# A third buffer for the radial weights and for the hops' one-hots, and one landing wait per sixteen gathers, in a four-layer graph network

## The chip, the cores and the metric

The kernel runs on one core of one Trainium2 chip. The time is the device time of that core in microseconds, from the start of the program to its end. Lower is better. The times come from repeated executions of one compiled program. The profile comes from one further execution.

## The reference

A graph has 6,250 nodes with 64 features and 200,000 edges (source, target, 32 and 4 edge features, two edge types). Four layers run one after the other, each with a residual and a layer norm:

```python
x = _layernorm(x + _L0_gnn_ref(...))   # radial = silu(edge_attr @ w1 + b1) @ w2 + b2: 1024 weights per edge;
                                       # message = tensor product of x[src], the edge harmonics and these weights;
                                       # segment_sum over dst, divided by the source degree
x = _layernorm(x + _L1_gnn_ref(...))   # relational layer: 8 bases, coefficients by edge type, segment_sum over dst
x = _layernorm(x + _L2_gnn_ref(...))   # h = x @ weight; out = segment_sum(h[row] * norm, col) + bias
x = _layernorm(x + _L3_gnn_ref(...))   # two hops; each gathers head, tail and relation rows, works out
                                       # hyperbolic maps per edge, and sums relu(res) over head
```

What matters here is that every layer gathers a row per edge, works on it, and sums it into the rows of nodes.

## The kernel before

**Edges in order.** A first stage ranks the edges by target and by source and writes them into slots, padded so that a group of 256 slots belongs to one chunk of 128 nodes. There are 1,664 tiles of 128 edges. BT = 16 tiles make a block, so there are 104 blocks. A sum over nodes is a matmul: a one-hot matrix of the edges' lanes (128 edges by 128 nodes, made by VectorE with an is_equal against a row of numbers) is the stationary operand, the messages are the moving one, and VectorE adds the 128 x 64 result to the accumulator of nodes in SBUF.

**Layer one** (product_phase). Four engines work on a block at once:

- SyncE loads the block's edge records (l_rec) when VectorE has given the buffer back (rec_used). In the first 50 blocks it also waits there for the scatters that GpSimd issues (rcb_sent) before it reloads their source, and the load of the next block's records is queued behind that.
- GpSimd copies the indices (line 666), issues 16 indirect DMAs that gather the source rows (line 671), waits for all 16, makes the features feat in eight operations (lines 680 to 687), and in the first 50 blocks issues 16 scatters of other records (line 693).
- TensorE turns four tiles of hidden features at a time (lines 727 and 729; ScalarE copies them out, line 713) and makes the 1,024 radial weights of a tile with four matmuls of 512 columns (line 737, function tile). They go to p_rad, which has two buffers of two PSUM banks; tile j may start when VectorE has read tile j-2 (semaphore tile_done). At the end of a block it makes the first two tiles of the next block, then waits for the block's messages (msg_done) and sums them with 16 products (line 761), which the trace shows as 32 matmuls.
- VectorE multiplies each tile's weights by the features (lines 800 and 802), reduces (line 809), and after 16 tiles makes the messages (lines 841 to 845) and the next block's one-hots (line 793). The sums of the last block are added (line 854) between the tiles 2 to 9 of the next one.

**Layer three** (spread_phase). Per block GpSimd issues 16 gathers (line 1101) and waits after each eight until they have all landed. TensorE sums them (line 1115), VectorE makes one-hots (line 1131) and adds (line 592). There are four buffers of gathered rows and of indices; VectorE copies the indices of block b + 4 when the sums of block b are made (line 1141).

**The hops** (hop_phase, twice). A pass handles 64 tiles in four units of 16, and there are 26 passes in a hop. GpSimd gathers the tail rows (line 1458, a wait after each eight). TensorE picks head and relation rows by matmul (lines 1476 and 1480, function pick), ScalarE copies them out (lines 1516 and 1517), and VectorE works through the hyperbolic formulas. Then, unit by unit, VectorE finishes the messages (lines 1779 to 1787), ScalarE applies the relu (line 1539), VectorE makes two halves of edge one-hots (function hots, line 1587, halves m = 0 to 7) in two buffers, TensorE sums a half as soon as its one-hots stand (line 1494), and VectorE adds unit u - 2 (add_unit, line 592). Half m may be written when the sums of half m - 2 are made (sum_done). After the last unit VectorE prepares the next pass with products of the tails and of the heads (lines 1596 and 1611), for which it waits until ScalarE has copied the picked rows.

The order on each engine is the order in which the code is written; semaphores tie the engines together.

## Time and profile before

| | us |
|---|---|
| median of 3 runs | 23192.35 |
| lowest and highest run | 23182.50, 23208.56 |
| the profiled execution | 23174.65 |
| its span, first to last instruction | 23172.8 |
| VectorE busy | 15518.0 (67%) |
| GpSimd busy | 12776.2 (55%) |
| TensorE busy | 10208.4 (44%) |
| ScalarE busy | 2702.6 (12%) |

No engine is busy all the time, so each stage has to be read for itself. Layer one lies between about 3560 and 10440 us, layer two between 10440 and 13250, layer three between 13640 and 16230, and the two hops between 16470 and 23172. The share of busy time in a window tells which engine is nearest to being the bound of a stage, the list of waits tells what an engine waited for, and the timeline shows in which order it happened.

### The profile page before, as it was taken

How to read it: one execution, taken by the hardware profiler on the slowest of the kernel's cores; microseconds unless marked ns; L12 is line 12 of the kernel's file. 1: busy time of each engine (PE TensorE's matmuls, PEld its weight loads, DVE VectorE, ACT ScalarE, POOL GpSimd, SP SyncE). 2: the span in 40 equal slices, each digit the busy share in tenths (PEclk: the TensorE clock that was granted, in tenths of full speed). 3: DMA queues.
4: the chain of work that ended last, by engine and by line, in shares of the span. 5: the costliest groups of instructions: out<-in, count | busy, mean ns of one | idle time of the engine just before them, and what ended most of it. 6: DMA issues, size and time to landing. Idle time of an engine off the chain costs nothing. (4 is left out here: it accounts for less than half of the span.)

```text
span 23172.8 us, 208220 instructions
## 1 busy us (share of the span) xinstructions
PE 10208.4 (44%) x47565; PEld 6761.2 (29%) x47566; DVE 15518.0 (67%) x25810; ACT 2702.6 (12%) x6634; POOL 12776.2 (55%) x12678
## 2 busy tenths in 40 slices
PE   0033335655555555555666632222234434344333
PEld 0033332222222222222222332222233333233333
DVE  8744447998888888887666521111477777677777
ACT  0011110000000000000000000000122332223322
POOL 0188886666565656644666426665355554455553
PEclk9999996555555555557888755555555555555555
DMA  4033331111111111111111101111422222222222
GB/s 176 21 69 69 70 69 28 24 24 24 23 22 23 22 24 21 24 22 22 24 24 24 17 13 21 21 21 20 59 61 61 56 58 51 58 63 60 57 59 47
DMA packets 1151509, 957.47 MB, mean 41 GB/s; under 512 B 803963, under 2 KB 920315, under 8 KB 1150739
## 3 DMA queue, kind: packets, MB, share of 16 engines
q0 software_dynamic: 419904, 437.84, 11.0%
q1 hardware_dynamic: 730960, 512.22, 8.6%
q8 instruction: 260, 4.26, 0.1%
q14 instruction: 385, 3.15, 0.0%
HBM read 734.68 MB, written 210.63 MB: 41 GB/s over the span
## 5 line engine op out<-in xcount | busy, mean ns | idle before, releaser
L1458 POOL DMA_INDIRECT tail<-ball,h_idx x3328 | 3445.4, 1035 | 3295.5 <-issue 1379.1
L737 PE MATMUL p_rad<-w_stack,hid_t 99*128 99x512 bf16 (+1 forms) x6656 | 3073.8, 619 | 2355.2 <-DVEq L827 1082.5
L1494 PE MATMUL h_sum<-head,h_hot 128*128 128x64 f32 x6656 | 1446.7, 417 | 3475.0 <-ACT head L1539 2117.5
L809 DVE TENSOR_REDUCE red<-prod 128x96 f32<-128x1536 f32 x1664 | 2900.2, 1743 | 3.5
L1494 PEld LDWEIGHTS h_sum<-head,h_hot 128*128 128x128 f32 x6656 | 1414.0, 327 | 3500.3 <-issue 3500.3
L1101 POOL DMA_INDIRECT l_xg<-h_tab,l_idx x1664 | 1573.9, 946 | 1462.7 <-issue 957.6
L338 POOL DMA_INDIRECT rec_a<-rec,slot x1600 | 1988.9, 1243 | 517.0 <-issue 501.4
L693 POOL DMA_INDIRECT rec_b<-l_rcb x1600 | 1929.8, 1206 | 570.9 <-issue 514.6
L932 POOL DMA_INDIRECT l_xg<-x_tab,l_idx x1664 | 1574.2, 946 | 1154.2 <-issue 834.1
L948 PE MATMUL l_sum<-outer,l_hot 128*128 128x512 f32 x3328 | 1684.6, 670 | 971.1 <-DVEq L993 899.5
L737 PEld LDWEIGHTS p_rad<-w_stack,hid_t 99*128 99x128 bf16 (+1 forms) x6656 | 773.3, 132 | 4300.7 <-issue 4298.8
L800 DVE TENSOR_TENSOR prod<-p_rad,feat 128x768 f32<-128x768 f32 x1664 | 1581.4, 950 | 545.4 <-remote 279.1
L671 POOL DMA_INDIRECT l_xg<-in_x,l_idx x1664 | 1581.9, 951 | 524.7 <-issue 475.6
L802 DVE TENSOR_TENSOR prod<-p_rad,feat 128x768 f32<-128x768 f32 x1664 | 1576.1, 947 | 0.0
L1115 PE MATMUL l_sum<-l_xg,l_hot 128*128 128x64 f32 x3328 | 734.1, 422 | 1880.5 <-DMA l_xg<-h_tab,l_idx 1880.5
L358 PE MATMUL p_all<-w_all,kinds 97*125 97x40 f32 x3200 | 691.1, 409 | 1637.7 <-DVEq L413 1637.7
L983 DVE TENSOR_TENSOR outer<-l_pcoef,l_xg 128x1024 f32<-128x1024 f32 x832 | 1015.3, 1220 | 527.4 <-DMA l_xg<-x_tab,l_idx 461.5
L1141 DVE COPY l_idx<-src_a 128x16 uint32 x100 | 18.5, 185 | 1914.0 <-PE l_sum L1115 1355.3
L948 PEld LDWEIGHTS l_sum<-outer,l_hot 128*128 128x128 f32 x3328 | 711.8, 218 | 1943.3 <-issue 1943.3
L1115 PEld LDWEIGHTS l_sum<-l_xg,l_hot 128*128 128x128 f32 x3328 | 717.6, 332 | 1897.1 <-issue 1897.1
L1476 PE MATMUL h_head<-ball_parts,hot_t 128*128 x9984 | 1032.3, 271 | 406.7 <-issue 300.2
L713 ACT ACTIVATE hid_t<-l_turn 96x1024 bf16<-96x1024 bf16 x416 | 424.4, 1020 | 6572.0 <-PE l_turn L729 3956.0
(368 smaller groups left out, 18411.8 us busy)
## 6 DMA issues: line engine op xcount, KB each, us to landing
hot_t<-rows_l SPq DMA_DIRECT2D x208, 512.0 KB
rec_a<-fill SPq DMA_DIRECT2D x128, 728.0 KB, 19.6
l_rec<-rec_a SPq DMA_DIRECT2D x104, 896.0 KB, 4.8
rhot_t<-rows_r SPq DMA_DIRECT2D x208, 384.0 KB
tail<-ball,h_idx POOLq DMA_INDIRECT x3328
t<-in_type SPq DMA_DIRECT2D x100, 500.0 KB
l_xg<-in_x,l_idx POOLq DMA_INDIRECT x1664
l_xg<-x_tab,l_idx POOLq DMA_INDIRECT x1664
```

Source lines behind the costliest of these rows:

```text
L338: pool.indirect_dma_start(rec_a[:, :], bass.IndirectOffsetOnAxis(ap=slot[q][:, j:j + 1], axis=0), rec[q][:, j, :], None).then_inc(sent[q], 16)
L671: pool.indirect_dma_start(xg[q][:, j, :], None, x[:, :], bass.IndirectOffsetOnAxis(ap=idx[q][:, j:j + 1], axis=0)).then_inc(gathered[q], 16)
L693: pool.indirect_dma_start(rec_b[:, :], bass.IndirectOffsetOnAxis(ap=rcb[q][:, j, 3:4].bitcast(U32), axis=0), rcb[q][:, j, :], None).then_i ...
L737: ins = pe.matmul(p_rad[j % 2][:, h * 512:(h + 1) * 512], hid_t[j // 4 % 2][0:K3 + 3 * (1 - i), j % 4, i, :], w_stack[i][0:K3 + 3 * (1 - i ...
L800: ch.step(dve.tensor_tensor(o[:, 0:48, :].rearrange("p (a w) u -> p a w u", a=3), w[:, 0:3], bc(f[:, j, 0:3, :].unsqueeze(2), [P, 3, MUL, ...
L802: ch.step(dve.tensor_tensor(o[:, 48:96, :].rearrange("p (w i) u -> p w i u", i=3), bc(w[:, 3].unsqueeze(2), [P, MUL, 3, MUL]), bc(f[:, j, ...
L809: ch.step(dve.tensor_reduce(red[:, j, :], prod[j % 3][:, :, :], AX, ALU.add))
L932: pool.indirect_dma_start(xg[u][:, j, :], None, table[:, :], bass.IndirectOffsetOnAxis(ap=idx[u][:, j:j + 1], axis=0)).then_inc(gathered[u ...
L948: ins = pe.matmul(p_sum[k % 4][:, :], hot[q][:, 2 * k + j, :], outer[k % 3][:, j, :, :].rearrange("p b d -> p (b d)"), start=(j == 0), sto ...
L1101: pool.indirect_dma_start(xg[u][:, j, :], None, table[:, :], bass.IndirectOffsetOnAxis(ap=idx[u][:, j:j + 1], axis=0)).then_inc(gathered[u ...
L1458: pool.indirect_dma_start(tg[q][:, j, :], None, table[:, :], bass.IndirectOffsetOnAxis(ap=idx[q][:, j:j + 1], axis=0)).then_inc(gathered[q ...
L1494: ins = pe.matmul(p_sum[u % 2][:, j % BT // 2, :], hot[j // HP8 % 2][:, j % HP8, :], hg[:, j, 0:D], start=(j % 2 == 0), stop=(j % 2 == 1))
```

## The change

Three edits that don't touch each other. In layer one p_rad gets a third buffer (all eight PSUM banks are then in use), tile j waits for VectorE's reading of tile j - 3, or for the last tile of the block before in the case of tile 0, and TensorE makes three tiles instead of two of the next block before it turns to the sums. In layer three GpSimd waits once per 16 gathers, and the copies of the indices move from VectorE to ScalarE, which has nothing else to do there. In the hops the one-hots of the edges get a third buffer, so half m waits for the sums of half m - 3.

```diff
-        p_rad = [ps(f"p_rad{q}", [P, COLS]) for q in range(2)]
+        p_rad = [ps(f"p_rad{q}", [P, COLS]) for q in range(3)]
...
-                hold(pe, turn, tile_done, b * BT + (j + 1))
+                hold(pe, turn, tile_done, b * BT + (3 if j == 0 else j if j < 3 else j + 1))
...
-                        ins = pe.matmul(p_rad[j % 2][:, h * 512:(h + 1) * 512], hid_t[j // 4 % 2][0:K3 + 3 * (1 - i), j % 4, i, :],
+                        ins = pe.matmul(p_rad[j % 3][:, h * 512:(h + 1) * 512], hid_t[j // 4 % 2][0:K3 + 3 * (1 - i), j % 4, i, :],
...
                 tile(b, 1)
+                tile(b, 2)
...
-                for j in range(2, BT):
+                for j in range(3, BT):
...
-            dve.sem_inc(tile_done, SEED)
+            dve.sem_inc(tile_done, 3)
...
-                w = p_rad[j % 2][:, :].rearrange("p (a w u) -> p a w u", a=4, u=MUL)
+                w = p_rad[j % 3][:, :].rearrange("p (a w u) -> p a w u", a=4, u=MUL)
...
             act.activation(p_row[:, 0:P], g["row"][:, :], ACT.Copy).then_inc(row_ready, 1)
+            for u in range(4):
+                act.activation(idx[u][:, :], g["src_a"][:, u * BT:(u + 1) * BT], ACT.Copy).then_inc(idx_ready, 1)
+            with act.Fori(0, NB // 4 - 1) as it:
+                for u in range(4):
+                    b = it * 4 + u
+                    hold(act, turn, sum_done, b + 1)
+                    act.activation(idx[u][:, :], g["src_a"][:, bass.ds((b + 4) * BT, BT)], ACT.Copy).then_inc(idx_ready, 1)
...
-                        if j % 8 == 7:
-                            hold(pool, turn, gathered[u], it * (16 * BT) + 16 * (j + 1))
+                    hold(pool, turn, gathered[u], it * (16 * BT) + 16 * BT)
...
-            for u in range(4):
-                dve.tensor_copy(idx[u][:, :], g["src_a"][:, u * BT:(u + 1) * BT]).then_inc(idx_ready, 1)
...
-                if left == 2:
-                    dve.tensor_copy(idx[u][:, :], g["src_a"][:, bass.ds((b + 4) * BT, BT)]).then_inc(idx_ready, 1)
...
-        hot = [sb(f"h_hot{k}" + tag, [P, HP8, P]) for k in range(2)]
+        hot = [sb(f"h_hot{k}" + tag, [P, HP8, P]) for k in range(3)]
...
-                        ins = pe.matmul(p_sum[u % 2][:, j % BT // 2, :], hot[j // HP8 % 2][:, j % HP8, :], hg[:, j, 0:D],
+                        ins = pe.matmul(p_sum[u % 2][:, j % BT // 2, :], hot[j // HP8 % 3][:, j % HP8, :], hg[:, j, 0:D],
...
-                if m >= 2:
-                    dve.wait_ge(sum_done, b * (2 * HU) + (m - 1))
-                ch.do(tt(hot[m % 2][:, :, :], lane3, bc(ends[q][:, 0, z].unsqueeze(2), [P, HP8, P]), ALU.is_equal))
+                if m >= 3:
+                    dve.wait_ge(sum_done, b * (2 * HU) + (m - 2))
+                ch.do(tt(hot[m % 3][:, :, :], lane3, bc(ends[q][:, 0, z].unsqueeze(2), [P, HP8, P]), ALU.is_equal))
```

On TensorE, at the end of a block of layer one (the names carry their buffer numbers: l0_hot0 and l0_sum belong to the block that ends, l0_rec1 and p_rad to the next one), before:

```order
L737 MATMUL p_rad0<-w_stack1,hid_t0 128x512 x2
L727 MATMUL l0_turn<-l0_ident_b,l0_rec1 96x128 [waits l0_kept]
L729 MATMUL l0_turn<-l0_ident_b,l0_rec1 96x128
...
L74 REGISTER_ALU
L737 MATMUL p_rad1<-w_stack0,hid_t0 128x512 [waits l0_tile_done]
L737 MATMUL p_rad1<-w_stack0,hid_t0 128x512
L737 MATMUL p_rad1<-w_stack1,hid_t0 128x512 x2
L761 MATMUL l0_sum<-msg,l0_hot0 128x64 [waits l0_msg_done,l0_added]
L761 MATMUL l0_sum<-msg,l0_hot0 128x64 x15
L74 REGISTER_ALU
L737 MATMUL p_rad0<-w_stack0,hid_t0 128x512 [waits l0_tile_done]
```

The same place now:

```order
L74 REGISTER_ALU
L737 MATMUL p_rad1<-w_stack0,hid_t0 128x512 [waits l0_tile_done]
L737 MATMUL p_rad1<-w_stack0,hid_t0 128x512
L737 MATMUL p_rad1<-w_stack1,hid_t0 128x512 x2
L74 REGISTER_ALU
L737 MATMUL p_rad2<-w_stack0,hid_t0 128x512 [waits l0_tile_done]
L737 MATMUL p_rad2<-w_stack0,hid_t0 128x512
L737 MATMUL p_rad2<-w_stack1,hid_t0 128x512 x2
L762 MATMUL l0_sum<-msg,l0_hot0 128x64 [waits l0_msg_done,l0_added]
L762 MATMUL l0_sum<-msg,l0_hot0 128x64 x15
L74 REGISTER_ALU
```

Tile 2 of the next block, with its wait for tile_done, has moved from behind the sums to ahead of them.

On GpSimd, in layer three (l_xg are the gathered rows, l_idx their indices), two blocks before:

```order
L1101 DMA l_xg<-h_tab,l_idx 128x64 [waits h_idx_ready]
L1101 DMA l_xg<-h_tab,l_idx 128x64 x7
L1101 DMA l_xg<-h_tab,l_idx 128x64 [waits l2_gathered1]
L1101 DMA l_xg<-h_tab,l_idx 128x64 x7
L74 REGISTER_ALU [waits l2_gathered1]
L1101 DMA l_xg<-h_tab,l_idx 128x64 [waits h_idx_ready]
L1101 DMA l_xg<-h_tab,l_idx 128x64 x7
```

and now:

```order
L1109 DMA l_xg<-h_tab,l_idx 128x64 [waits h_idx_ready]
L1109 DMA l_xg<-h_tab,l_idx 128x64 x15
L74 REGISTER_ALU [waits l2_gathered1]
L1109 DMA l_xg<-h_tab,l_idx 128x64 [waits h_idx_ready]
L1109 DMA l_xg<-h_tab,l_idx 128x64 x15
```

The wait in the middle of a block is gone, the one at its end has stayed.

## Rows read from the trace of the kernel before

**Rows 1.** Windows by stage (layer one, layer three); columns stand in the first line.

```profile
core 0: us, PE busy (x) PEld busy (x) DVE busy (x) ACT busy (x) POOL busy (x), PEclk, DMA share, GB/s
3560.00:10440.00 6880.00, 4046.84 (x13112) 1848.47 (x13112) 6167.48 (x6137) 419.25 (x411) 4183.57 (x4400) 0.52 0.13 23
...
13640.00:16230.00 2590.00, 731.34 (x3316) 715.00 (x3317) 431.89 (x1028) 0.00 (x0) 1570.33 (x1661) 0.50 0.14 21
```

**Rows 2.** Groups by line, GpSimd's gathers of layer three and scatters of layer one.

```profile
L1101 POOL DMA_INDIRECT l_xg<-h_tab,l_idx x1664 | 1573.9, 946 | 1462.7 <-issue 957.6 <-DVE l_idx L1123 452.9 <-DMA l_xg<-h_tab,l_idx 52.2
...
L693 POOL DMA_INDIRECT rec_b<-l_rcb x1600 | 1929.8, 1206 | 570.9 <-issue 514.6 <-POOL feat L687 56.3
```

**Rows 3.** Timeline of GpSimd in layer three: start, us, idle before and its releaser.

```profile
15011.35 0.95 POOL L1101 DMA_INDIRECT l_xg<-h_tab,l_idx  x1 [0.30 <-issue]
15014.99 0.94 POOL L1101 DMA_INDIRECT l_xg<-h_tab,l_idx  x1 [2.69 <-issue]
...
15027.42 0.95 POOL L1101 DMA_INDIRECT l_xg<-h_tab,l_idx  x1 [2.74 <-issue]
```

**Rows 4.** Timeline of TensorE in layer one, from a block's end into the next.

```profile
6019.41 1.91 PE L737 MATMUL p_rad<-w_stack,hid_t 99*128 99x512 bf16 x4
6026.33 7.06 PE L761 MATMUL l_sum<-msg,l_hot 128*128 128x64 f32 x32 [5.01 <-DVEq L846]
6033.18 3.58 PE L737 MATMUL p_rad<-w_stack,hid_t 99*128 99x512 bf16 x8
...
6044.20 1.87 PE L737 MATMUL p_rad<-w_stack,hid_t 99*128 99x512 bf16 x4 [1.65 <-DVEq L827]
```

**Rows 5.** Timeline of VectorE in the same block: L800 starts a tile.

```profile
6035.13 0.96 DVE L800 TENSOR_TENSOR prod<-p_rad,feat 128x768 f32<-128x768 f32 x1 [1.51 <-issue]
...
6038.66 0.95 DVE L800 TENSOR_TENSOR prod<-p_rad,feat 128x768 f32<-128x768 f32 x1
...
6042.18 0.95 DVE L800 TENSOR_TENSOR prod<-p_rad,feat 128x768 f32<-128x768 f32 x1
...
6053.64 0.96 DVE L800 TENSOR_TENSOR prod<-p_rad,feat 128x768 f32<-128x768 f32 x1 [4.14 <-remote]
```

**Rows 6.** Timeline of GpSimd in the same block: last gather, then the features.

```profile
6049.86 0.95 POOL L671 DMA_INDIRECT l_xg<-in_x,l_idx  x1 [0.30 <-issue]
6052.39 1.50 POOL L680 TENSOR_TENSOR vec<-l_xg,l_rec 128x768 f32<-128x768 f32 x1 [1.58 <-DMA l_xg<-in_x,l_idx]
```

**Rows 7.** VectorE's waits in layer one, from 3600 to 4880 us: total, times, longest.

```profile
DVE prod L800 <- remote: 3.8, 1, 3.8
```

**Rows 8.** The same from 4950 to 10440 us.

```profile
DVE prod L800 <- remote: 275.2, 73, 4.6
DVE prod L800 <- issue: 109.0, 72, 3.2
```

**Rows 9.** GpSimd in layer one's first blocks: start of a block's index copy.

```profile
3638.29 0.20 POOL L666 CAST l_idx<-l_rec 128x16 uint32<-128x16 f32 x1 [7.05 <-DMA l_rec<-rec_a]
...
3892.56 0.21 POOL L666 CAST l_idx<-l_rec 128x16 uint32<-128x16 f32 x1 [7.10 <-DMA l_rec<-rec_a]
```

**Rows 10.** Timeline of VectorE in a pass of the first hop.

```profile
18126.94 1.23 DVE L1587 TENSOR_TENSOR h_hot<-h_row,h_ends 128x1024 f32<-128x1024 f32 x1 [1.86 <-PE h_sum L1494]
...
18139.64 2.60 DVE L1587 TENSOR_TENSOR h_hot<-h_row,h_ends 128x1024 f32<-128x1024 f32 x2 [6.16 <-PE h_sum L1494]
...
18166.88 2.76 DVE L592 TENSOR_TENSOR acc_nodes<-acc_nodes,h_sum 128x64 f32 x8 [2.98 <-PE h_sum L1494]
...
18193.47 0.69 DVE L1596 TENSOR_TENSOR h_hot<-head,h_rhot 128x512 f32<-128x512 f32 x1 [3.89 <-ACT head L1517]
```

**Rows 11.** TensorE in the same pass, the sums of the second unit.

```profile
18131.29 7.06 PE L1494 MATMUL h_sum<-head,h_hot 128*128 128x64 f32 x32 [2.23 <-issue]
```

**Rows 12.** GpSimd in the same pass, the last gather of an eight.

```profile
18137.09 0.95 POOL L1458 DMA_INDIRECT tail<-ball,h_idx  x1 [0.30 <-issue]
```

**Rows 13.** What VectorE's one-hots of both hops waited for: us, times.

```profile
  PE h_sum L1494: 262.6, 132
```

## Prediction made before the run

> **What bounds the kernel now.** I read the windows by stage first, since the busy shares of the whole span are an average over stages with different limits, and then, for each stage that the change touches, the groups by line, the waits and the timelines of the engines that wait.
>
> Layer three is GpSimd's stage: of 2590 us in the window TensorE is busy 731, VectorE 432 and GpSimd 1570 [rows 1]. The 1664 gathers have 1462.7 us of idle time before them [rows 2]. 452.9 of that is one wait at the start of the stage. The rest, 1009.8, is the 0.30 us that stands before each gather anyway, and the wait for landing after each eight, 2.69 and 2.74 us in the block that I looked at [rows 3].
>
> In layer one VectorE is busy for 6167 of 6880 us [rows 1]. It takes a tile each 3.52 us (6038.66 to 6042.18) and stalls twice in most blocks [rows 5]. The first stall is before tile 2 of a block, 1.51 us: TensorE makes tiles 0 and 1, waits 5.01 us for the messages, makes the sums (6026.33 to 6033.39) and only then tile 2 [rows 4]. The second is before tile 6, 4.14 us, released by something that the profile only calls remote. TensorE's matmuls of that tile end at 6046.07 [rows 4], while VectorE starts at 6053.64 [rows 5]. That moment is 3.78 us after the start of the last of the block's 16 gathers, at 6049.86 [rows 6]. In the later blocks such a wait stands 73 times with 275.2 us, and the late wait for tile 2 72 times with 109.0 us [rows 8]; in the first twenty blocks a remote wait stands once [rows 7]. I read it so: TensorE's signal for a tile whose matmuls end while the gathers are being issued is held until they are through. It fits the times; it isn't shown.
>
> In the first 50 blocks GpSimd issues scatters too. Four blocks take 254.27 us there, 63.6 each, paced by its own round (records in, gathers, features, scatters) [rows 9]. By the blocks that I counted, blocks 21 to 49 take about 67.7 us each: there the gathers have come into step with VectorE's stall. That number is from the whole timeline of the stage, and its own stalls (1.5 and 3.8 us over the 63.6) make nearly the same.
>
> In the hops VectorE has gaps at the one-hots (1.86 us before half 3, 6.16 us before half 4), at the sums of the last unit (2.98) and at the head products (3.89) [rows 10]. Over both hops the one-hots wait 262.6 us for TensorE, 132 times [rows 13]. The matmuls that free half 4's buffer are the first half of the 7.06 us from 18131.29 on [rows 11], so they end near 18134.8; VectorE goes on at 18139.64, 2.55 us after the start of an eight's last gather at 18137.09 [rows 12]. This is the same kind of late signal.
>
> **Layer three's waits.** 1664 gathers in 104 blocks have 104 waits in mid-block and 103 at block ends that count. 1009.8 less 1457 x 0.305 = 444 leaves 565 for 207 waits, 2.73 us each, as the two rows show [rows 3]. A gather without the wait stands 0.30 behind the one before it. So the edit takes 104 x (2.73 - 0.305) = **252 us**. The index copies that move to ScalarE cost nothing: it does nothing in this window [rows 1], and each of its four buffers is refilled three blocks ahead of its use. What is late next? TensorE's sums need 731/104 = 7.0 us of a block, VectorE 4.2, and a block would last 22.2 us, so GpSimd stays the bound. The price on the other side is that 16 gathers in flight might be issued or land more slowly than eight. In layer one 16 gathers run back to back with 0.30 us between them, and the last has landed 2.53 us after its start (6049.86 to 6052.39) [rows 6], against 3.64 from start to next gather after eight in layer three (15011.35 to 15014.99) [rows 3]. So I take the full 252. Its bounds are 104 x 2.2 = 229, if the longer run of gathers makes the one remaining wait 0.23 us longer, and 265, if the mid-block waits are a little longer than those at the ends.
>
> Here the Trainium skill bears on the trace. Its page "DMA: Bandwidth & Descriptors", in the section "Anatomy of one DMA — SWDGE (gpsimd) path", puts a fixed 2.0 us on each DMA that GpSimd issues, most of it the time until the write is confirmed and the semaphore may rise. By that page 104 waits would be worth an estimated 208 us. The rows measure what stands in the way of GpSimd, 2.73 us, and the sum goes by them.
>
> **Layer one's third buffer.** No instruction is added but one wait per block that changes its count; tile 2 of the next block moves ahead of the sums. Does it fit there? With three buffers tile 0 waits for the last product of the block, which is where tile 1 waits today (6019.41). Three tiles of 1.91 us are 5.7 us, and the messages come at 6026.33, 6.9 us later [rows 4]; 1.2 us are left for the turns, which are short. So the sums aren't delayed, and the 1.51 us before tile 2 goes. If the cover were short by 1 us, the sums would start so much later, but VectorE needs them only between its tiles 2 and 9, so nothing waits.
>
> What does the second stall do? VectorE comes to tile 6 some 1.5 us earlier, and with three buffers TensorE makes tile 6 one tile (3.52 us) earlier still, so that its matmuls end near 6041 instead of 6046. I take it that this is early enough to be signalled before the hold. Then tile 7 is the one caught: VectorE wants it one tile later than tile 6 and gets it when the hold ends, at the same distance from the gathers as now. So per stalled block the gain isn't the whole 1.5 + 4.1 but **one tile, 3.52 us**. By stretches:
> - blocks 0 to 20: GpSimd's round of 63.6 us sets the pace, nothing is gained;
> - blocks 21 to 49: from 67.7 down to at best GpSimd's 63.6, 29 x 4.1 = 119 us (3.52 by the rule above and a part of it that the gathers' new place gives back);
> - blocks 50 to 103: no scatters, 54 x 3.52 = 190 us.
>
> Sum **309 us**. The bounds are wide, since the held signal is inferred. If only the wait before tile 2 goes, 103 x 1.5 = 155. If the signal's end alone sets the pace of a block, VectorE arriving earlier only waits longer, and about 20 is left. If the stall is gone altogether, the second half gains 54 x (1.5 + 4.1) = 302 and the middle 119 to 160, up to 460.
>
> **The hops' third buffer.** Half m waits for the sums of half m - 3. The gaps of 1.86 (half 3) and 6.16 us (half 4) go, but half 5 then waits for what half 4 waits for today, the signal at 18139.6. Half 4's one-hots are one of the two in the 2.60 us row [rows 10], so 1.3 us per pass are made beside the wait. By this 52 x 1.37 = 71 us, and with the gap of half 3 fully counted 52 x 3.3 = 172. Against it: later in the pass VectorE waits 2.98 us for TensorE and 3.89 for ScalarE's copy of the head rows [rows 10]. Those are set by TensorE's order and by the gathers, not by VectorE, and swallow what came before them in about half of the passes. The next picks by TensorE aren't earlier when VectorE is. I take **50 us**, with 0 and 172 as bounds.
>
> **The sum.** 252 + 309 + 50 = 611 us. 23174.65 - 611 = 22563.65 for the profiled execution, which lies 17.7 us under the median of the runs and 1.85 over its span. For the median I add the 17.7 back, 22581, and say 22580.
>
> **Rivals.**
> - *Only the wait before tile 2 goes in layer one.* The stall at tile 6 then stays as long as it is, because the hold is tied to VectorE's own place in the block: the gathers start when VectorE gives the records back, and move with it. Gain 155 + 252 + 20 = 427, so 22765. The steady 3.78 us between gather and release speaks for it, the earlier end of tile 6's matmuls against.
> - *The stall of layer one vanishes.* If the hold catches only what ends in the last part of the gathers, and tile 7 slips past as well, then 460 + 252 + 100 = 812, so 22380. For it speaks that tiles 3, 4 and 5 come without a wait while gathers are issued too [rows 5].
> - *The edit in layer one does not do what it says.* The held signal sets the block's period and VectorE only waits longer: 20 + 252 + 20 = 292, so 22900. For it: GpSimd's gathers begin when VectorE has given the buffer back, and the release comes a fixed time behind them. Against it: the 1.51 us stall stands ahead of that point in the block.
> - *Slower.* Sixteen gathers in flight without a wait may be issued at the pace of the scatters of layer one, which also come sixteen in a row, 1206 ns and 0.30 apart [rows 2], against 0.95 and 0.30 [rows 3]. Then 1664 x 0.25 = 416 us are added in layer three and 252 saved, 164 slower. With layer one and the hops swallowed to nothing the time is 23192 + 164 = 23356. From 0.15 us more per gather (252/1664) the edit has lost its gain. Against it: layer one's gathers, sixteen in a row too, take 0.95 [rows 6].
>
> **How the numbers follow.** The case of the sum has 0.50, the rival with only tile 2's wait 0.20, the vanished stall 0.15, the swallowed edit 0.10, the slower one 0.02, and 0.03 is left for mixtures near no change. The predicted time is the first case's. The range runs from 22370, which takes in the vanished stall, to 22830, which takes in the case with only tile 2's wait at its upper bound of the hops' zero (22785) and some of the way to the swallowed edit; what is left out is most of that case, the slower one and tails, under 2 in 10. About 0.2%, 46 us, is what a measurement of this kernel can tell from no change: faster by more than that has 0.96, within it 0.02, slower 0.02.
>
> **What would show it.** In layer three the idle time before the gathers falls from 1463 to about 1210 us, no gap stands in mid-block, the gathers stay at 0.95, and a block lasts 22.2 us. In layer one VectorE has no wait before tile 2 of a block, the stall at tile 6 is gone and one of about 2.6 us stands before tile 7, and the stage is 309 us shorter. If the second stall keeps its 4 us at tile 6, the step on the earlier signal was wrong; if the stage gains nearly nothing, the step that VectorE sets the gathers was. In the hops the one-hots' wait for TensorE falls from 262.6 us by half or more, and the waits at the sums (2.98) and at the head products (3.89) grow. The prediction is wrong as a whole if the gathers' mean duration rises in layer three, or if the wait at a block's end grows by the 2.4 us that the middle one gave.

## The result

The changed kernel took 22420.81 us (median of 4 runs, 22394.77 to 22503.10), the kernel before 23200.46 in the runs beside it (23182.50 to 23209.55). The ratio is **0.967, with a 95% interval from 0.9645 to 0.9697**. The profiled execution went from a span of 23172.8 to 22392.9 us, 780 us less, where the sum had 611.

The windows of the two stages stand first, as in [rows 1].

```profile
core 0: us, PE busy (x) PEld busy (x) DVE busy (x) ACT busy (x) POOL busy (x), PEclk, DMA share, GB/s
3560.00:10100.00 6540.00, 3840.07 (x13280) 1821.07 (x13280) 6282.49 (x6227) 424.48 (x416) 4343.93 (x4408) 0.56 0.14 24
13200.00:15610.00 2410.00, 803.08 (x3296) 771.68 (x3296) 420.99 (x929) 21.56 (x100) 1571.23 (x1663) 0.50 0.15 23
```

VectorE is now busy for 6282 of 6540 us of layer one, 96%, against 90%. From the first to the last product the stage lasts 6495.2 us, before 6928.6: 433 less. Layer three lasts 2405.0 us from its first to its last gather, before 2583.7: 179 less. The hops last 6290.7 us from the first to the last one-hots, before 6457.8: 167 less. The three make the 780; the other stages are within 3 us.

**Layer one.** VectorE's waits from 4950 to 10000 us, the products' own (us in total, times, longest), against [rows 8]:

```profile
DVE prod L801 <- PE p_rad L737: 35.0, 70, 1.3
...
DVE prod L801 <- POOLq L688: 0.8, 1, 0.8
```

The 275.2 us of remote waits and the 109.0 us before tile 2 have gone, both. What is left is 0.5 us before tile 10, which the kernel before has too. In the timeline of VectorE and GpSimd in one block (start, us) the tiles stand one behind the other, and the gathers start late in the block:

```profile
6981.73 0.95 DVE L801 TENSOR_TENSOR prod<-p_rad,feat 128x768 f32<-128x768 f32 x1
6983.46 0.95 DVE L801 TENSOR_TENSOR prod<-p_rad,feat 128x768 f32<-128x768 f32 x1
6986.85 0.95 DVE L801 TENSOR_TENSOR prod<-p_rad,feat 128x768 f32<-128x768 f32 x1
...
7004.44 0.95 DVE L801 TENSOR_TENSOR prod<-p_rad,feat 128x768 f32<-128x768 f32 x1
```

```profile
7010.64 0.20 POOL L666 CAST l_idx<-l_rec 128x16 uint32<-128x16 f32 x1 [6.99 <-DMA l_rec<-rec_a]
...
7011.62 0.99 POOL L671 DMA_INDIRECT l_xg<-in_x,l_idx  x1 [0.48 <-POOL lane_a L668]
```

The first gather comes 29.9 us behind the block's first product (7011.62 less 6981.73). In the kernel before it came 2.6 us behind it from block 20 on; there it had started at 32.7 and drifted. In the changed kernel it stays between 29.8 and 33.0 us in blocks 0 to 97; then the gathers jump, within three blocks, to 2.5 us. From block 20 on a block lasts 62.5 us, before 67.5.

**Layer three.** The gathers' group, against the first of [rows 2], and one block's end on GpSimd, against [rows 3]:

```profile
L1109 POOL DMA_INDIRECT l_xg<-h_tab,l_idx x1664 | 1572.3, 945 | 1285.8 <-issue 614.3 <-ACT l_idx L1096 453.0 <-ACT l_idx L1101 165.2
```

```profile
14528.14 0.94 POOL L1109 DMA_INDIRECT l_xg<-h_tab,l_idx  x1 [0.30 <-issue]
14534.11 0.95 POOL L1109 DMA_INDIRECT l_xg<-h_tab,l_idx  x1 [5.02 <-ACT l_idx L1101]
```

The idle time has fallen by 177 us, not by 252. No wait stands in mid-block, but 165.2 us are new, waits for ScalarE's index copies. ScalarE copies when TensorE's sums are made, and in TensorE's timeline the sums now look like this:

```profile
14539.01 7.06 PE L1122 MATMUL l_sum<-l_xg,l_hot 128*128 128x64 f32 x32 [5.00 <-DVEq L1138]
14551.47 4.85 PE L1122 MATMUL l_sum<-l_xg,l_hot 128*128 128x64 f32 x21 [5.39 <-issue]
...
14560.39 0.27 PE L1122 MATMUL l_sum<-l_xg,l_hot 128*128 128x64 f32 x1 [0.25 <-issue]
14561.11 0.46 PE L1122 MATMUL l_sum<-l_xg,l_hot 128*128 128x64 f32 x1 [0.45 <-issue]
14562.52 0.27 PE L1122 MATMUL l_sum<-l_xg,l_hot 128*128 128x64 f32 x1 [0.95 <-issue]
...
14565.36 0.27 PE L1122 MATMUL l_sum<-l_xg,l_hot 128*128 128x64 f32 x1 [1.65 <-issue]
14573.13 0.87 PE L1122 MATMUL l_sum<-l_xg,l_hot 128*128 128x64 f32 x3 [7.50 <-issue]
```

The first block's 32 matmuls take 7.06 us, as those of every block did in the kernel before. The next block's start well, 21 in 4.85 us, and then come one by one, 0.70 or a multiple of it apart (14560.39, 14561.11, 14562.52), with nothing in the profile that they wait for. Counted over the stage, the sums take 7.1 us in 38% of the blocks and 9 to 40 us in the others, 17.7 on average. VectorE's register instructions last 0.70 us each in many places of these stretches, where 0.04 to 0.06 is usual. It isn't the loading of code: the trace has four packets of instructions in the whole stage, in either kernel. So a block lasts 23.16 us on average, and only the median, 22.37, is near the forecast 22.2.

**The hops.** What VectorE waited for there (us in total, times, longest), first before, then after:

```profile
DVE h_hot L1587 <- PE h_sum L1494: 272.2, 139, 6.3
...
DVE acc_nodes L592 <- PE h_sum L1494: 130.8, 38, 5.0
...
DVE h_hot L1587 <- remote: 128.8, 28, 6.2
```

```profile
DVE acc_nodes L592 <- PE h_sum L1497: 218.3, 32, 9.4
DVE acc_nodes L592 <- remote: 139.9, 25, 10.1
...
DVE h_hot L1590 <- PE h_sum L1497: 79.7, 51, 4.8
```

The one-hots' waits fall from 8.7 to 2.9 us per pass, those before the additions rise from 8.6 to 12.4, those before the head and tail products fall from 5.4 to 4.0. By half: before half 3 the wait went from 1.73 to 0.18, before half 4 from 4.00 to 0.15, and before half 5 it stayed (1.36 and 1.33). All that was added before the additions stands in one place, before those of the last unit: 3.68 us per pass became 7.46. In one pass, VectorE at half 5, TensorE's sums of halves 2 and 3, and GpSimd's gathers around them:

```profile
17824.56 1.22 DVE L1590 TENSOR_TENSOR h_hot<-h_row,h_ends 128x1024 f32<-128x1024 f32 x1 [1.30 <-PE h_sum L1497]
```

```profile
17820.88 7.06 PE L1497 MATMUL h_sum<-head,h_hot 128*128 128x64 f32 x32 [2.16 <-issue]
```

```profile
17824.26 0.94 POOL L1461 DMA_INDIRECT tail<-ball,h_idx  x1 [0.30 <-issue]
17825.51 0.94 POOL L1461 DMA_INDIRECT tail<-ball,h_idx  x1 [0.30 <-issue]
```

The first half of the 7.06 us ends at 17824.4, in the middle of a run of gathers, and VectorE goes on at 17824.56. In [rows 10] and [rows 11] the same matmuls ended at 18134.8, and VectorE went on at 18139.64.

### The profile page after: what moved, and what is told of

Read it like the earlier page. It is cut to its first block and busy times, and to the rows that moved or that the text cites. A ratio compares the mean times of both kernels' runs of the same rounds, so it can differ in the third digit from the quotient of the medians.

```text
span 22392.9 us, 208316 instructions
## 1 busy us (share of the span) xinstructions
PE 9998.2 (45%) x47565; PEld 6760.8 (30%) x47566; DVE 15533.6 (69%) x25706; ACT 2711.3 (12%) x6738; POOL 12929.4 (58%) x12678
## 5 line engine op out<-in xcount | busy, mean ns | idle before, releaser
L737 PE MATMUL p_rad<-w_stack,hid_t 99*128 99x512 bf16 (+1 forms) x6656 | 2879.5, 589 | 2470.7 <-DVEq L828 1094.6
L693 POOL DMA_INDIRECT rec_b<-l_rcb x1600 | 2065.7, 1291 | 570.8 <-issue 514.5
L1122 PE MATMUL l_sum<-l_xg,l_hot 128*128 128x64 f32 x3328 | 810.1, 394 | 1629.3 <-issue 1319.0
L592 DVE TENSOR_TENSOR acc_nodes<-acc_nodes,l_sum 128x64 f32 x832 | 183.6, 221 | 1884.3 <-remote 1500.5
L1122 PEld LDWEIGHTS l_sum<-l_xg,l_hot 128*128 128x128 f32 x3328 | 778.6, 320 | 1660.8 <-issue 1659.8
L358 PEld LDWEIGHTS p_all<-w_all,kinds 97*125 97x125 f32 x3200 | 679.4, 330 | 1646.7 <-issue 1646.7
```

The source lines that it names most:

```text
L693: pool.indirect_dma_start(rec_b[:, :], bass.IndirectOffsetOnAxis(ap=rcb[q][:, j, 3:4].bitcast(U32), axis=0), rcb[q][:, j, :], None).then_i ...
L737: ins = pe.matmul(p_rad[j % 3][:, h * 512:(h + 1) * 512], hid_t[j // 4 % 2][0:K3 + 3 * (1 - i), j % 4, i, :], w_stack[i][0:K3 + 3 * (1 - i ...
L1122: ins = pe.matmul(p_sum[u % 2][:, j // 2, :], hot[u % 2][:, j, :], xg[u][:, j, :], start=(j % 2 == 0), stop=(j % 2 == 1))
```

## The experiments

The kernels ran in four groups, after the runs of the result, each group on one chip and together with the kernel before, which didn't take the same time in all: 22907 us in the first group, 22848 in the second, 22470 and 22468 in the third and fourth. So every ratio stands against the runs of its own group, and part of the answer is what differs between the groups. The kernel before has a profile in none of them; where its stages are needed, they are taken from a kernel of the group that leaves them as they are.

### One edit at a time

Each kernel is the kernel before with one of the three edits, word for word as in the change.

> The kernel before with the third buffer of radial weights alone. In the changed kernel layer one lasts 433 us less (6928.6 to 6495.2 us from its first to its last product). Theory S (the three edits are independent, each in its own stage): 433 us faster, 1.9%, a ratio of 0.981. Rival (the stages disturb each other, or the late signals depend on something that another edit changed): under 350 us, and VectorE's stall before tile 6 is seen again.

> The kernel before with the edit of layer three alone. In the changed kernel that stage lasts 179 us less (2583.7 to 2405.0 us from the first to the last gather), 73 less than forecast, because the waits at the ends of blocks have grown from 2.63 to 3.47 us. Theory S: 179 us faster, 0.8%, and again sums of 30 us and more beside sums of 7.1 us, with end waits near 5 us behind them. Rival (the long sums come from the state in which the chip reaches the stage): 252 us faster and all sums at 7.1 us.

> The kernel before with the third buffer of one-hots in the hops alone. Theory S: 163 us faster, 0.7%. The prediction had 50 (bounds 0 and 172), and the idle time before the one-hots falls from 8.7 to 2.9 us per pass while that before the sums' additions rises by 3.9. Rival (part of the gain in the hops came from elsewhere): 50 to 100 us.

| kernel | median us | ratio to before (22907.37) | interval | its own stage against the same stage in another kernel of the group |
|---|---|---|---|---|
| layer one's buffer | 22662.82 | 0.9891 | 0.9874 to 0.9907 | 6543.3 against 6802.1: 259 less |
| layer three's edit | 22710.47 | 0.9909 | 0.9892 to 0.9925 | 2392.2 against 2587.1: 195 less |
| the hops' buffer | 22755.80 | 0.9932 | 0.9916 to 0.9949 | 6166.5 against 6330.3: 164 less |

Each gain stands in its own stage, so the edits look independent, though no run of this group has all three together. Layer three's edit alone brings the slow sums (17.7 us on average again). The hops' 164 is close to the 167 that the full change gave. Layer one's edit gave 259, not 433: the number is the rival's (under 350), but the stall before tile 6 that the rival expected isn't seen in it. The reason is on the other side: in the two kernels of this group that leave layer one as it was, the stall before tile 6 is 1.8 to 1.9 us in place of 3.6. The gain of that buffer goes with the stall that it finds.

### More work for GpSimd, to move the gathers

```diff
                 ch.sync()
+                if scattering:
+                    for _ in range(2):
+                        ch.do(pool.tensor_tensor(v4, x1, bc(sh1.unsqueeze(2), [P, BT, MUL, 3]), ALU.mult))
                 ch.do(pool.tensor_tensor(f[:, :, 1, :], v4[:, :, :, 0], v4[:, :, :, 1], ALU.add))
```

> The kernel before, and GpSimd repeats one product of the features twice (1.5 us each) in the 100 blocks of layer one that scatter; nothing else is changed, and all values stay the same. In the kernel before GpSimd's gathers drift within 20 blocks from 33 us behind a block's first product to 2.6 us behind it, and the stall before tile 6 (3.5 to 3.8 us) begins there. Theory P (the stall needs the gathers to lie at the start of a block, together with TensorE's sums and VectorE's additions; GpSimd gets ahead because its round is shorter than VectorE's 63.8 us): with 3 us more of its own work GpSimd stays near 30 us behind, the stall never comes, a block lasts 63.8 to 64.8 us in place of 67.5, and the added work makes the kernel 200 to 300 us faster. Rival H (TensorE's signals are held during any late part of the gathers, as the prediction had it): the stall only moves to another tile, the time stays within 50 us or grows by up to 300.

Measured: 23057.17 us, ratio 1.0067 (1.005 to 1.0083), 150 us slower. VectorE's product waits from 4950 to 9800 us:

```profile
DVE prod L803 <- POOLq L691: 192.5, 73, 5.5
...
DVE prod L803 <- PE p_rad L740: 37.4, 72, 0.7
```

and in its last blocks (10290 to 10540 us), where the scatters have ended:

```profile
DVE prod L803 <- PE p_rad L740: 8.8, 8, 1.6
...
DVE prod L803 <- remote: 2.7, 1, 2.7
```

The gathers stay 32.4 to 32.9 us behind the first product, and with two buffers the stall before tile 6 is 0.00 in 99 blocks. In the last blocks of the same run the gathers come 2.4 us behind it, and the stall is back, with a remote wait of 2.7 us. So the stall needs the gathers at the start of the block, theory P on the mechanism, and H, the rule of the prediction, falls: with the gathers elsewhere it went to no other tile. The time that P gave was wrong. The round of GpSimd grew to 67.0 us, since its features (now 15.4 us from the last gather to the first scatter, before 8.9; 3.0 of that are the two products at their usual length) fall on VectorE's messages and one-hots, and both get slower: the one-hots take 3.2 us in place of 2.29. VectorE waits 2.6 us per block for the features.

### The changed kernel again

No edit.

> The changed kernel as it is, beside the kernel before, to have both on the chip on which the next runs are made. Where the kernel before has the longer stall before tile 6 of layer one (3.7 us, 23192 us in all) the ratio was 0.967. On the chip of the single edits, where that stall was 1.9 us and the kernel before took 22907 us, the three gains sum to 2.7%. Theory (the third buffer takes what stall there is): 0.965 to 0.975, and the more the slower the kernel before is. Rival (a further gain only when all three stand together): 0.967 on any chip.

Measured: 22332.44 us against 22847.83, ratio 0.9774 (0.9756 to 0.9791). Its interval doesn't touch the first one, so the rival, one ratio everywhere, is out: the change is worth 780 us where the kernel before takes 23200, and 515 where it takes 22848. The theory's range (0.965 to 0.975) was a little too low as well. The changed kernel itself moved by 88 us only, the kernel before by 353.

### Layer three: when the waits stand, and how much TensorE does

In the first kernel the end wait of three of four blocks stands after the eighth gather of the next block, in the second TensorE makes half of the products.

```diff
+                        if j == 7 and u > 0:
+                            hold(pool, turn, gathered[u - 1], it * (16 * BT) + 16 * BT)
-                    hold(pool, turn, gathered[u], it * (16 * BT) + 16 * BT)
+                    if u == 3:
+                        hold(pool, turn, gathered[u], it * (16 * BT) + 16 * BT)
```

```diff
-                    for j in range(BT):
+                    for j in range(0, BT, 2):
-                        ins = pe.matmul(p_sum[u % 2][:, j // 2, :], hot[u % 2][:, j, :], xg[u][:, j, :], start=(j % 2 == 0),
-                                        stop=(j % 2 == 1))
+                        ins = pe.matmul(p_sum[u % 2][:, j // 2, :], hot[u % 2][:, j, :], xg[u][:, j, :], start=True, stop=True)
```

> The changed kernel, and in layer three GpSimd doesn't wait at the end of three of four blocks; it waits for those gathers after the eighth of the next block, when they have long landed. Up to 24 gathers are then under way. Theory Q (the sums of 20 to 45 us come from a backlog that gathers build up when nothing stops them for more than about ten in a row, and that a wait clears): with fewer stops TensorE's sums stay slow in nearly all blocks, TensorE becomes the bound of the stage, and the stage gains nothing or gets longer by up to 300 us. Rival N (sums are slow beside gathers, but GpSimd stays the bound): 78 end waits of 2.4 us or more go, the stage is 190 us or more shorter, a ratio 0.008 below that of the changed kernel.

> The changed kernel with half of layer three's sums left out (8 products for a block in place of 16). Theory Q2 (the slow stretches need both the gathers' run of sixteen and a dense row of short instructions on TensorE and VectorE): the slow stretches get fewer or vanish, the end waits fall from 3.5 towards 2.4 us, and the stage is up to 75 to 110 us shorter than in the changed kernel, a ratio 0.003 to 0.005 lower. Rival (the gathers alone do it): end waits stay at 3.5 us on average and the stage at 2400 us.

Measured: 22356.32 us, ratio 0.9780 (0.9763 to 0.9796), and 22363.36 us, ratio 0.9786 (0.977 to 0.9802); the changed kernel has 0.9774 in this group. The gathers' groups of the changed kernel, of the one with rolling waits and of the one with half the sums:

```profile
L1109 POOL DMA_INDIRECT l_xg<-h_tab,l_idx x1664 | 1574.0, 946 | 1267.7 <-issue 646.5 <-ACT l_idx L1096 452.6 <-ACT l_idx L1101 123.4
```

```profile
L1109 POOL DMA_INDIRECT l_xg<-h_tab,l_idx x1664 | 1574.0, 946 | 1265.8 <-issue 487.4 <-ACT l_idx L1096 452.5 <-ACT l_idx L1101 313.5
```

```profile
L1109 POOL DMA_INDIRECT l_xg<-h_tab,l_idx x1664 | 1574.0, 946 | 1250.5 <-issue 671.0 <-ACT l_idx L1096 453.9 <-ACT l_idx L1101 79.7
```

Moving 78 end waits to where their gathers should have landed gives back 2 us of the stage (2389.2 to 2387.3). The time goes from the landing waits (issue, 646.5 to 487.4) to the wait for the index copies (123.4 to 313.5), that is, for TensorE's sums: every second block's take some 30 us. A wait takes the place of the one removed, as theory Q has it, though the stage got no longer. With half the products the sums take 3.65 us in all blocks, yet 17 of 103 end waits are still over 4 us (26 in the changed kernel of the group), VectorE's register and semaphore instructions over 0.55 us are more, not fewer (1287 against 703 in that kernel), and the stage is 19 us shorter, not 75: the dense row of matmuls isn't what brings the slow stretches. The block lasts 22.8 to 23.2 us in all the versions so far, the single edit too, which made me think of a rate.

### The same edit in layer two

```diff
-                        if j % 8 == 7:
-                            hold(pool, turn, gathered[u], it * (16 * BT) + 16 * (j + 1))
+                    hold(pool, turn, gathered[u], it * (16 * BT) + 16 * BT)
```

> The changed kernel with the same edit in layer two as well: one landing wait for sixteen gathers. In the changed kernel that stage's gathers have 1148 us of idle time, 507 of it their own spacing, so its 207 waits cost 3.1 us each, and VectorE is busy for 1735 to 2000 of some 2600 us. Theory G (GpSimd is the bound there too): 104 waits of 2.4 us less, 250 us faster than the changed kernel, ratio 0.011 lower, less 75 if slow stretches come as in layer three. Rival V (VectorE's chain behind the gathers or the index copies behind it are the bound, and the slow stretches hit 32 products of 512 columns per block): within 60 us of the changed kernel, or slower.

Measured: 22604.99 us, ratio 0.9889 (0.9872 to 0.9905), 273 us slower than the changed kernel. Gathers and matmuls of layer two, first of the changed kernel, then of this one:

```profile
L933 POOL DMA_INDIRECT l_xg<-x_tab,l_idx x1664 | 1574.0, 946 | 1150.2 <-issue 897.3 <-DVE l_idx L957 131.1 <-DMA l_xg<-x_tab,l_idx 121.8
...
L949 PE MATMUL l_sum<-outer,l_hot 128*128 128x512 f32 x3328 | 1677.5, 668 | 979.9 <-DVEq L994 878.5 <-issue 101.4
```

```profile
L933 POOL DMA_INDIRECT l_xg<-x_tab,l_idx x1664 | 1573.9, 946 | 1358.7 <-DVE l_idx L999 714.8 <-issue 488.6 <-DVE l_idx L956 131.1
...
L948 PE MATMUL l_sum<-outer,l_hot 128*128 128x512 f32 x3328 | 1860.5, 718 | 1042.4 <-issue 564.3 <-DVEq L995 280.5 <-DVEq L993 140.5
```

GpSimd now waits 714.8 us for the index copies of VectorE, which stand behind a chain of additions that wait for sums; TensorE has 564.3 us of idle time that nothing explains, before 101.4; a block's sums take 21.8 us in place of 16.1. The wait before a block's first gather, index copies included, is 7.3 us on average, before 2.7. It is rival V: the engines behind the gathers are nearer to their bound here (the sums alone 16 of 25 us, not 7), so the slow stretches decide.

### Where the gathers lie, and how many in a row

The first kernel is the kernel before with a wait on SyncE (the counts of tile_done are raised by 16 to keep them positive), the second the kernel before with a landing wait after the eighth gather of layer one.

```diff
                 sp.wait_ge(rec_used, b + 1)
+                sp.wait_ge(tile_done, b * BT + (SEED + 3))
```

```diff
+                    if j == 7:
+                        hold(pool, turn, gathered[q], it * (16 * BT) + 16 * 8)
                 hold(pool, turn, gathered[q], it * (16 * BT) + 16 * BT)
```

> The kernel before (two buffers of radial weights) with one more wait on SyncE: the records of the next block are loaded only when VectorE has done three tiles of a block. Nothing is added to GpSimd or VectorE. This keeps GpSimd's gathers near 18 to 20 us behind a block's first product, away from the block's start, without the 3 us of work (and the slower features and messages) that the run with the repeated product had. Theory P (the stall before tile 6 comes only where the gathers lie at a block's start): it is gone, only the 1.5 us before tile 2 and the 0.5 before tile 10 are left, a block lasts 63.9 to 64.5 us in place of 65.7 (or 67.5 on a slow chip), 120 to 300 us faster than the kernel before. Rival H (late signals go with any late part of sixteen gathers): the stall moves to tile 10 or 11 with the same size, within 40 us of the kernel before.

> The kernel before with a landing wait after the eighth gather in layer one as well (it had one per sixteen there); GpSimd has time to spare in that stage. Theory B (late signals and slow stretches need more than eight gathers in a row): the stall before tile 6, 1.9 to 3.7 us per block, is gone, 130 to 290 us faster. Rival (the landing wait has no part in it): within 50 us of the kernel before, the stall stays, a little later in the block.

Measured: 22472.20 us, ratio 1.0001 (0.9991 to 1.001), and 22724.09 us, ratio 1.0112 (1.0095 to 1.0129). Product waits from 4950 to 9800 us of the one, then of the other:

```profile
DVE prod L801 <- PE p_rad L738: 154.0, 153, 1.5
```

```profile
DVE prod L802 <- POOLq L690: 217.6, 73, 4.1
DVE prod L802 <- PE p_rad L739: 38.1, 73, 0.7
```

With the gate the gathers come 14.7 us behind the first product and a block lasts 63.6 us, with the waits before tile 2 and tile 10 and no other, as P says. But the kernel before took as long in this group, 22470 us, so it had no stall to remove, and the run decides nothing between P and H. The second kernel shows why: its last blocks have their gathers 2.6 us behind the first product, two buffers, and a wait before tile 6 of 0.00; in the first group such blocks had 1.2 to 1.7. The hops, where both groups run the same code with a wait after each eight gathers, say the same. When VectorE waits for a half's sums before half 4, it goes on 2.1 us after their matmuls have ended in the first group (3.4 in the profile before), and 0.04 us after in this one. In this group the late signals aren't seen anywhere. So theory B can't be tested on the stall here. For the rest the mid-block wait does harm: it makes GpSimd's round nearly as long as the repeated products did (66.3 and 67.1 us; the gathers stay at 32.7), and VectorE waits 3.0 us per block for the features. I had held that GpSimd has time to spare in that stage, and it has not.

### Records first, and a lagged wait

Two edits to the changed kernel, in two stages: SyncE loads the next block's records before it waits for the scatters, and in layer three the first eight gathers have a semaphore of their own, half, for which GpSimd waits after the twelfth. The second kernel has that wait in the first 52 blocks only.

```diff
+            load(0, 0)
             with sp.Fori(0, SB // 2 - 1) as it:
                 for q in range(2):
-                    load(it, q)
+                    load(it + q, 1 - q)
                     sp.wait_ge(rcb_sent[q], it * (16 * BT) + 16 * BT)
...
+                        if j == 11:
+                            hold(pool, turn, half[u], it * (8 * BT) + 8 * BT)
```

> The changed kernel with two edits in two stages, to be read by stage. Layer one: SyncE loads the next block's records before it waits for the scatters. GpSimd's round gets 8 us shorter than VectorE's 62.4, so its gathers move to the start of VectorE's block, where the stall was, now with three buffers. Theory T (the third buffer takes the late signals by itself): stalls of at most 1.5 us per block, a block of 62.4 to 63.5 us, the stage within 60 us of the changed kernel. Theory P2 (the stall is gone from the changed kernel because its gathers stay 30 us behind): 2 to 4 us per block come back, the stage 150 to 350 us longer. Layer three: the first eight gathers have a semaphore of their own and GpSimd waits for them after the twelfth, when they should have landed. Depth theory (a backlog builds because nothing bounds the gathers under way): slow sums vanish, a block lasts 22.2 us, the stage 80 us shorter. Rate theory (sixteen gathers take some 22.9 us of something shared, whatever the waits, as the runs with 22.8, 23.0, 23.0 and 23.2 us per block suggest): 22.8 to 23.2 us again.

> The changed kernel with the records of layer one loaded first (as in the run before), and in layer three the lagged wait after the twelfth gather in the first 52 blocks only; the last 52 have one wait per sixteen gathers, as the changed kernel. In the last call the kernel before took 22470 us, against 22850 to 23200 earlier, and neither the stall of layer one nor a slow sum was seen in it, so what the lagged wait did is open. Theory W (the lagged wait keeps the sums fast): 7.1 us in the first half of layer three and 20 to 45 us in about 60% of the blocks of the second, whatever the kernel before takes. Theory S2 (the late signals and the slow sums belong to the state the chip is in): both halves alike, all at 7.1 us if the kernel before is near 22470 us, both with slow sums if it is near 22900 or 23200. Layer one: with the kernel before near 22900 or above, third buffer enough by itself (theory T): stalls under 1.5 us per block and 62.0 to 63.5 us per block; otherwise (P2) 2 to 4 us per block come back.

Measured: 22041.71 us, ratio 0.9807 (0.979 to 0.9823), and 22040.52 us against 22467.52, ratio 0.9810 (0.9793 to 0.9826). Of the second kernel: the gathers of the last 52 and of the first 52 blocks of layer three, and TensorE's sums in the last 52.

```profile
L1121 POOL DMA_INDIRECT l_xg<-h_tab,l_idx x832 | 785.0, 943 | 404.5 <-issue 404.5
...
L1112 POOL DMA_INDIRECT l_xg<-h_tab,l_idx x832 | 784.9, 943 | 832.7 <-ACT l_idx L1099 451.9 <-issue 363.6 <-DMA l_xg<-h_tab,l_idx 17.2
```

```profile
14957.00 7.06 PE L1135 MATMUL l_sum<-l_xg,l_hot 128*128 128x64 f32 x32 [15.60 <-DMA l_xg<-h_tab,l_idx]
14979.40 7.06 PE L1135 MATMUL l_sum<-l_xg,l_hot 128*128 128x64 f32 x32 [15.34 <-DMA l_xg<-h_tab,l_idx]
```

All 104 sums take 7.1 us, in both halves. So it isn't the lagged wait that keeps them fast, and theory W falls. The number of the depth theory, 22.2 us for a block, wasn't met either (22.7 in the first kernel). In the last two groups neither late signals nor slow sums are there. The rate, too, falls as a general limit: with the waits of the changed kernel a block lasts 22.5 us in blocks 52 to 77, less than the 22.7 to 23.0 that the versions before had in the same blocks. The edit of layer three with its lagged wait is worth 228 us here (2355.2 us of the stage against 2583.6 in the kernel with the gate), against 179 and 195 where the sums are slow. The hops, with three buffers, last 6049 and 6046 us against 6073 and 6066 with two: 20 us, where they gave 164 and 167. The wait before half 4 that the buffer removes is 1.1 to 1.2 us there, against 3.0 in the first group and 4.0 in the profile before.

Layer one with the records first takes 6438 us, a block 62.0 us. GpSimd no longer waits for the records in its first rounds, which take 54 us, and within four blocks its gathers come 2.5 to 3.2 us behind the first product, as in the kernel before. The messages and one-hots no longer meet GpSimd's features (scatters of 1190 ns on average against 1279 to 1291 in the changed kernel). In groups with late signals this was not run, so whether the third buffer is enough with the gathers there stays open. The last blocks of the six kernels with three buffers that ran where signals were late are all there is on it: the gathers lie 2.5 us behind, and the waits before tiles 6 and 7 are 0.0 to 1.7 us per block, 1.0 on average, against 1.2 to 1.9 before tile 6 with two. Nearly all of it stands before tile 7. That speaks for a part only.

This version has the lowest time of all, and layer one's part of it is below the changed kernel's in every profile. But the two never ran in the same group, so how much it gains over the changed kernel isn't measured.

## Why the prediction was right, and where it was not

The forecast was 22580 us with a range from 22370 to 22830; 22421 is in it. The sign and the order of the size were right. The terms were off by 73 us too much and by 124 and 117 too little, so the sum, off by 169, is better than its parts. In the profiled executions:

| term | forecast | measured | in the first group, alone |
|---|---|---|---|
| layer three's waits | 252 | 179 | 195 |
| layer one's buffer | 309 | 433 | 259 |
| the hops' buffer | 50 | 167 | 164 |
| sum | 611 | 780 | 618 |

That the sum of the first group lies so near 611 is luck: none of its three terms does.

**Layer three.** Right: a wait of 2.7 us in mid-block goes, GpSimd stays the bound, the gathers keep their 0.95 us and 0.30 between. Mis-sized: the bound below, 229, rested on the one remaining wait growing by 0.23 us. The mid-block waits were 2.84 us on average, not 2.73, so 264 us went. But the wait at the end grew from 2.63 to 3.47, 0.84 us in each of 103 blocks, which takes back 86. Even where no sum is slow it is 3.0. And the step "what is late next" took TensorE's sums at the 7.0 us that they have beside runs of eight gathers. Beside runs of sixteen they take 17.7 on average, and the index copies, which I had costed at nothing since ScalarE is idle, wait for them: 165 us of the end waits. The evidence that I cited for the full gain, layer one's sixteen gathers, showed that they land in time; it said nothing on what they do to other engines. The Trainium skill's page "DMA: Bandwidth & Descriptors", section "Anatomy of one DMA — SWDGE (gpsimd) path", would have had an estimated 208 us; with the slow sums the runs gave 179 and 195, without them 228, so neither it nor the rows' 252 was met, though 208 lies nearer to all three.

**Layer one.** The wait before tile 2 is gone, as forecast, and TensorE's margin ahead of the sums was enough: it still waits 2.1 us for the messages. The step that failed is the one on the second stall. The forecast was that tile 7 would take the wait that tile 6 had; that needed the gathers to stay where they were. They didn't, and both waits went in full, 1.5 and 3.6 us per block: the gain of the rival "the stall vanishes", though not for its reason. What the runs showed in its place is that the gathers never come to the place where the signals are late. With two buffers and the gathers at 32.7 us there is no stall before tile 6 either (the run with the repeated products). In the last blocks of the changed kernel, where the gathers jump to 2.5 us, a part of it comes back, mostly before tile 7, the tile of the forecast, with up to 1.7 us and not 2.6. Why the gathers stay can be read from GpSimd's round while its features and scatters meet the end of VectorE's block: 55.2 us from the index copies to the last scatter and 7.4 us of waiting for the next records, 62.5 in all. That is less than VectorE's 63.8 us in the kernel before, so there the gathers drift. It is as much as VectorE's block has shrunk to, 62.5, so here they stay. The run with the records first bears it out: without the 7.4 us a round takes 54, and within four blocks the gathers are at the block's start.

Two premises of that step were wrong too. The text ahead of the prediction and the prediction speak of 50 blocks with scatters; it is 100 (1600 scatters at 16 a block, as [rows 2] could have told), and so the cut between blocks 21 to 49 and 50 to 103 had no ground: they last 67.7 and 67.4 us. And what paces the first blocks [rows 9] isn't GpSimd's round, 62.6 us on average in the first 18, but VectorE's block, 63.8, some 61.8 of work and 2.0 of waits. So these blocks gained too (1.1 us each), where the forecast had nothing.

**The hops.** Half 3 and half 4 came free, as forecast, and the waits before the additions grew. But half 5 didn't take the wait over: the step that failed is the one by which half 5 waits for the signal at 18139.6. The matmuls that this signal stands for end 18.7 us after the pass's first one-hots in both kernels. In the kernel before VectorE goes on 3.4 us after that end, with the third buffer 0.14 us after it. So the signal isn't late any more, though the gathers of that part of the pass lie within 2 us of where they lay and are being issued at that moment; why, no run shows. That about half of what is won goes to later waits held: the one-hots of half 6 come 6.2 us earlier, and a pass is 3.2 us shorter. I took 50 us; the runs gave 167, close to the upper bound of 172. The cost that moved to the additions is 201 of 301 us, and 74 came back before the head and tail products.

**The held signal.** That TensorE's signals come late beside gathers is seen in the rows. That this belongs to the code was taken for granted, and it is the largest error behind the right range, which was right also because the result was taken where the stalls are longest. The stall that layer one's buffer removes is 3.6 us in one set of runs, 1.8 in another, and none in a third; the kernel before takes 23200, 22907 and 22470 us with it. The change is worth 780 us in the first, 515 at 22848, and by its stages some 230 us in layer three, 20 in the hops and 1.5 us a block before tile 2 (150) in the third, 400 us in all, which is an estimate from stages and not a run. At 22470 us that would be a ratio of 0.982. The hops of the kernel before alone take 6458, 6330 and 6073 us in the three. Of the 7.6 us per pass between the first and the last of these, 3.2 stand before the head products (3.8 and 0.6) and 2.8 before half 4 (4.0 and 1.2).

The chances: faster by over 0.2% had 0.96 and happened. The case of the sum had 0.50; what came is nearer to the vanished stall, which had 0.15 (812 us; the runs gave 780).

## What to carry to other kernels

Before you cost the removal of a stall, ask what sets its place: here a shorter block kept another engine from running ahead, and the collision never took place. A wait that throttles a queue may shield the other engines, on some occasions at least: taking it away was a gain where the engine behind was busy for 7 of 25 us, and a loss of 273 us where it was busy for 16 of 25. Both were measured where slow stretches occur; what the second costs where they don't wasn't run. And compare a kernel with the one before in the same group only: here the same kernel took between 22468 and 23200 us.

## What the runs showed of the hardware

- Beside runs of sixteen gathers without a landing wait TensorE's matmuls can fall to one in 0.70 us (or a multiple) from 0.21, and VectorE's register instructions to 0.70 us each from 0.04 to 0.06. In blocks 55 to 69 of the changed kernel such a stretch begins some 7 to 10 us into a run of gathers, goes on through the next two runs and the landing waits of 2.4 to 2.8 us between them, and ends in a wait of some 5 us (33 of the 103 end waits are over 4 us).
- In layer three it wasn't seen with a wait per eight gathers, in any group. With a wait per sixteen it was there in the profiles of the first run and of two groups, and in none of the last two groups. A wait per eight is no full shield elsewhere. In the hops, with that wait in every kernel, TensorE has 156 to 239 gaps of 0.35 to 0.6 us that nothing explains in the ten profiles of the first runs and the first two groups, and 0 to 2 in the four of the last two groups.
- VectorE can go on long after the modelled end of the matmuls that it waits for: 4.3 to 7.8 us before tile 6 of layer one and 3.4 us before half 4 of the hops in the kernel before, 0.04 us before half 4 in the third group.
- What differs between the groups isn't known. It isn't the chip's number: two groups with the kernel before at 22907 and 22470 us ran on the same one. It isn't the pace of the transfers: a 2048-byte packet of layer three's gathers takes 198 to 200 ns in the first two profiles, 211 to 214 in the first two groups, 197 to 200 in the third and 214 in the fourth. Nor does the recording of a profile make the difference, since the executions without one differ between the groups as much.
- VectorE and GpSimd slow each other when VectorE's messages and one-hots meet GpSimd's features: the one-hots take 2.29 us alone and 3.2 us beside them, the same product of the features 1.50 alone and 2.4 on average.
